# Attention on one Trainium2 core: gathering the plain float32 products into five places a unit

## The chip, the core and the metric

The kernel runs on one core of one Trainium2 chip. The metric is the device time of one launch in microseconds. The engines are TensorE (PE; its weight loads are listed apart as PEld), VectorE (DVE), ScalarE (ACT), GpSimd (POOL) and SyncE (SP), which here issues nearly all DMAs. Each has its own instruction stream, and semaphores are all that orders one against another.

## The reference, cut to what matters

```python
q = xt @ Wq.T                                   # (B, T, D), B 16, T 512, D 256
qh = q.reshape(B, T, NH, dk)                    # 8 heads of 32
scores = scale * einsum('bhqd,bhkd->bhqk', qh, qh)
logits = (scores * cmask + (1.0 - cmask) * NEG) * rmask
attn = softmax(logits, axis=-1)
ctx = einsum('bhqk,bhkd->bhqd', attn, qh)
out = ctx @ Wo.T                                # then a mixture of 8 experts, top 2,
x = x + moe(out) + shared(out) * sigmoid(gate)  # and one shared expert
```

## The kernel before, in words

The program has three parts, one after the other: `attention` (to about 700 us), `experts`, and `shared`. Only `attention` is touched.

Attention works in 32 units: 16 batch entries, two units each, each unit with HG = 4 of the 8 heads. In a unit there are KB = 4 blocks `kb` of 128 keys, and in each block the four heads `g`. A pair (kb, g) issues two products on TensorE: `ps_e` (L557), the scores of unit u, 98 rows deep by 512 columns, and `ps_m` (L562), the same scores the other way round for unit u+2, of which DVE takes the maximum (L420) so that the exponentials of two units later can have it subtracted. Both use float32r operands; high and low parts are stacked in the rows. Each of the two has two PSUM banks, taken in turn: the product of pair t on `ps_e` waits until ACT has made the exponential (L337) of pair t-2, and that on `ps_m` until DVE has reduced pair t-2 (`max_done`, L561).

Between the pairs `step` in the tensor block places by hand all other work of TensorE. A part of it is in plain float32:
- `numerators` (L455), of the block before, at g = 1 of each kb: four products with 32 output rows each, side by side in the array's columns, eight instructions in all; at kb = 0 it is the last block of the unit before;
- `denominators` (L468), the sum of exponentials by a matrix of ones, once for blocks 0 and 1 (g = 3, kb = 3), once for blocks 2 and 3 of the unit before (g = 3, kb = 1);
- `turn_values` (L477), `turn_maxima` (L496) and `turn_rows` (L506), transposes against `ident`;
- `partial_logits` (L514) and `logits` (L521), small products for the gate of the experts.

`turn_rows`, `partial_logits` and `logits` are there in units with even n only. `project` (L485) and `out_rows` (L535, odd n only) are six float32r products each.

The denominators need e[0]+e[1] and e[2]+e[3] added first. `add_pair` (L148) does that: POOL adds all of pair 0 and half of pair 1, DVE the other half of pair 1 (L422), after its reduce of kb 1, g 1; the denominators of pair 1 wait for it (`pair_dve`, L465).

At the end of a unit DVE also has, in its stream: a reciprocal in quarters (L386), two of them in kb 3; the product `c_f` (L391); the small copy `keep_logits` (L430, even n), or, at the head of an even unit, `row_mask` and `row_neg` (L411, L412). Only then do the reduces of the next unit follow.

Of the kernel before, what the change touches and what calls it, by code (L numbers as in the profile page):

```python
def attention(nc, ctx, sems, keep, x, mask, wqT, woT, gates, attn):
# [13 lines left out]
    NU = NB * UPB  # L15
# [88 lines left out]
    def upto(eng, s, value):  # L104

        if not (isinstance(value, int) and value <= 0):
            eng.wait_ge(s, value)
# [27 lines left out]
    def known(i, n, off=0, lo=0, hi=NU):  # L135

        if isinstance(i, int):
            return lo <= RING * i + n + off < hi
        return True
# [234 lines left out]
    @block.vector  # L374
    def _(dve):
        def normalise(i, n, at):

            w, par = RING * i + n - 1, (n - 1) % 2
            if at < 0:
                return  # L380
            if at < PARTS:
                c = slice(at * T // PARTS, (at + 1) * T // PARTS)
                if at == 0:
                    dve.wait_ge(den_done, w + 1)
                    upto(dve, c_done, w)
                dve.reciprocal(den[par][:, c], den[par][:, c]).then_inc(rd_done, 1)  # L386
            elif at == PARTS:
                dve.wait_ge(rd_done, PARTS * (w + 1))
                dve.wait_ge(num_done, w + 1)
                upto(dve, c_split, w - 1)  # L390
                dve.tensor_tensor(c_f[par][:], num[par][:], den[par][:], ALU.mult).then_inc(c_done, 1)  # L391

        dve.memset(one_f[:], 1.0).then_inc(dve_set, 1)
        dve.wait_ge(dve_set, 1)
        dve.tensor_copy(one_row[:], one_f[:]).then_inc(setup, 1)
        dve.wait_ge(w_in, 32)
        dve.tensor_copy(wq_hi[:], wq_f).then_inc(w_split, 1)
        dve.tensor_copy(wo_hi[:], wo_f).then_inc(w_split, 1)
        dve.wait_ge(w_split, 2)
        dve.tensor_tensor(wq_lo[:], wq_f, wq_hi[:], ALU.subtract).then_inc(w_split, 1)  # L400
        dve.tensor_tensor(wo_lo[:], wo_f, wo_hi[:], ALU.subtract).then_inc(w_split, 1)

        def step(i, n):
            u = RING * i + n
            if n % 2 == 0 and known(i, n, 4):
                b, bp = 2 * i + (n + 4) // 2, n // 2
                dve.wait_ge(mask_in[bp], 16 * (i + 2))

                if known(i, n, 1):
                    dve.wait_ge(stack_in[(n + 1) % RING], 16 * STACK_DMAS * (i + (n + 1) // RING + 1))  # L410
                dve.tensor_copy(row_mask[bp][:], mask_b[bp][0:1, :]).then_inc(rows_done, 1)  # L411
                dve.tensor_scalar(row_neg[bp][:], mask_b[bp][0:1, :], -NEG, NEG, ALU.mult, ALU.add).then_inc(rows_done, 1)  # L412
            for kb in range(KB):
                for g in range(HG):
                    if known(i, n, 2):
                        w, par = u + 2, n % 2
                        dve.wait_ge(m_mm, (KB * w + kb) * HG + g + 1)
                        if kb == 0 and g == 0:
                            upto(dve, mt_mm, w - 1)
                        dve.reduce_max(maxcol[par][:, g * KB + kb:g * KB + kb + 1], ps_m[g % 2][:, :], AX.X).then_inc(max_done, 1)  # L420
                    if g == 1 and kb == 1 and known(i, n, -1):
                        add_pair(dve, u - 1, 1, slice(0, HG // 2), pair_dve)  # L422
                    if g % 2 == 1 and known(i, n, -1):
                        normalise(i, n, 2 * kb + g // 2 - KB)
                        if kb == KB - 1 and g == HG - 1:
                            normalise(i, n, PARTS)
                if kb == 3 and n % 2 == 0 and known(i, n, -4, hi=NU):
                    b = 2 * i + (n - 4) // 2
                    dve.wait_ge(lg_mm, b + 1)
                    dve.tensor_copy(keep["logits"][:, bass.ds(KT * b, KT), :],  # L430
                                    ps_o[:, KT * P:KT * (P + NE)].rearrange("p (h e) -> p h e", h=KT)).then_inc(lg_done, 1)

        run_units(dve, step, -4, 5)

    @block.tensor
    def _(pe):
# [10 lines left out]
        def numerators(u, n, kb):  # L447

            if kb == 0:

                upto(pe, num_done, u)
                upto(pe, v_done, u + 1)
            pe.wait_ge(e_done, (KB * u + kb + 1) * HG)
            for g in range(HG):
                last = nc.tensor.matmul(ps_num[g * DK:(g + 1) * DK, :], v[n % RING][:, kb, g, :], e[kb][:, g, :],  # L455
                                        start=(kb == 0), stop=(kb == KB - 1))
            last.then_inc(num_mm, 1)
# [14 lines left out]
        def turn_values(i, n):  # L472

            w, par = RING * i + n + 3, (n + 3) % 2
            pe.wait_ge(q_done, 2 * (w + 1))
            for k in range(KB):
                last = nc.tensor.transpose(ps_q[:, k * P:(k + 1) * P], q_f[par][:, k * P:(k + 1) * P], ident[:, :])  # L477
            last.then_inc(v_mm, 1)
# [9 lines left out]
        def turn_maxima(i, n):  # L488

            upto(pe, max_done, (RING * i + n + 2) * KB * HG)  # L490

            if n % 2 == 0:
                upto(pe, o_done, KT * (2 * i + (n - 4) // 2 + 1))
            else:
                upto(pe, lg_done, 2 * i + (n - 5) // 2 + 1)
            nc.tensor.transpose(ps_o[0:HG * KB, 0:P], maxcol[(n + 1) % 2][:, :], ident[:, :]).then_inc(mt_mm, 1)  # L496
# [41 lines left out]
        def step(i, n):  # L538
            u = RING * i + n
            if isinstance(i, int) and u == 0:  # L540

                pe.wait_ge(ones_in, 16 * RING)
                pe.wait_ge(gate_in, 16)
                pe.wait_ge(add_up_done, KB)
            for kb in range(KB):
                cols = slice(kb * P, (kb + 1) * P)
                if kb == 0 and known(i, n):
                    pe.wait_ge(maxrow_in[n % RING], 16 * (i + 1))
                if kb == 0 and known(i, n, 2):
                    pe.wait_ge(stack_in[(n + 2) % RING], 16 * STACK_DMAS * (i + 1 + (n + 2) // RING))  # L550

                before = ((u - 1, n - 1, KB - 1) if known(i, n, -1) else None) if kb == 0 else ((u, n, kb - 1) if known(i, n) else None)
                for g in range(HG):
                    if known(i, n):
                        tile = (KB * u + kb) * HG + g
                        upto(pe, e_done, tile - 1)
                        nc.tensor.matmul(ps_e[g % 2][:, :], kside[n][:, g, cols], qside[n][:, g, :], start=True, stop=True).then_inc(e_mm, 1)  # L557
                    if known(i, n, 2):
                        s2 = (n + 2) % RING
                        tile = (KB * (u + 2) + kb) * HG + g  # L560
                        upto(pe, max_done, tile - 1)  # L561
                        nc.tensor.matmul(ps_m[g % 2][:, :], qside[s2][0:MAXROW, g, cols], kside[s2][0:MAXROW, g, :], start=True, stop=True).then_inc(m_mm, 1)  # L562
                    if g == 0 and kb == 0 and known(i, n, 3):
                        turn_values(i, n)
                    if g == 0 and kb == 2 and known(i, n, 4):
                        project(i, n)
                    if g == 1 and before:
                        numerators(*before)
                    if g == 2 and kb == 0 and known(i, n, 1):
                        turn_maxima(i, n)  # L570
                    if g == 2 and kb in (1, 2) and n % 2 == 0 and known(i, n, -4, hi=NU):
                        turn_rows(i, n, kb - 1)
                    if g == 0 and kb == 3 and n % 2 == 0 and known(i, n, -4, hi=NU):
                        partial_logits(i, n)
                    if g == 2 and kb == 3 and n % 2 == 0 and known(i, n, -4, hi=NU):
                        logits(i, n)
                    if g == 2 and kb >= 2 and n % 2 == 1 and known(i, n, -3, hi=NU):
                        out_rows(i, n, kb - 2)
                    if g == 3 and kb == 1 and known(i, n, -1):
                        denominators(u - 1, 1)  # L580
                    if g == 3 and kb == 3 and known(i, n):
                        denominators(u, 0)

        run_units(pe, step, -4, 5)

# [821 lines left out]
```

## Time and profile before

| | us |
|---|---|
| median of 3 runs | 2069.23 (2065.56 to 2070.95) |
| span of the profiled execution, first to last instruction | 2067.4 |
| TensorE busy, whole span | 1920.6 (93%) |
| DVE busy, whole span | 1061.5 (51%) |
| TensorE busy between 300 and 400 us | 96.02 of 100 |
| DVE busy between 300 and 400 us | 83.32 of 100 |
| ACT, POOL busy between 300 and 400 us | 68.30, 64.45 of 100 |

The time of the profiled execution itself is not listed; its span stands 1.8 us below the median of the runs. The timeline gives start, duration and instruction; ends of matmuls are modelled and overlap the next start, so the distance from start to start is what a matmul costs. An idle time in square brackets names what ended it.

### The profile page before, as it was taken

The numbers are of one execution on the slowest core, as the hardware profiler recorded it, in microseconds if no ns is written. First come the engines' busy times: TensorE is split into PE (matmuls) and PEld (weight loads), VectorE is DVE, ScalarE is ACT, GpSimd is POOL, SyncE is SP. The second block draws the span as 40 slices with busy tenths as digits, with TensorE's granted clock in tenths as the row PEclk, the third lists the DMA queues.
The fourth block names the chain that finished last, engine by engine and source line by source line (L and its number), as shares of the span: only waits on it lengthen the run. The fifth ranks groups of instructions, "written<-read, shape, count | busy, mean of one in ns | idle before, by whom it ended". The sixth has DMA issues, their size and how long they took to land. (4 is left out here: it accounts for less than half of the span.)

```text
span 2067.4 us, 30281 instructions
## 1 busy us (share of the span) xinstructions
PE 1920.6 (93%) x10324; PEld 1418.9 (69%) x10325; DVE 1061.5 (51%) x1723; ACT 720.1 (35%) x1282; POOL 591.3 (29%) x433
## 2 busy tenths in 40 slices
PE   4999999999999836999999999799999999999996
PEld 2444444444444326999999999688888888888885
DVE  3788888787888455344443443444233332424333
ACT  1566666666666512324343332311101010101100
POOL 3556665666565413111111111001010100101010
PEclk9899999999999956999999999899999999999998
DMA  7765757576765033233332322523030211203021
GB/s 126 120 111 98 113 102 125 92 113 95 131 84 73 21 143 125 81 116 110 123 121 73 114 80 81 169 91 102 1 102 20 81 51 51 67 34 101 0 81 41
DMA packets 103041, 184.22 MB, mean 89 GB/s; under 512 B 10560, under 2 KB 31040, under 8 KB 102992
## 3 DMA queue, kind: packets, MB, share of 16 engines
q1 hardware_dynamic: 91952, 147.41, 32.3%
q0 software_dynamic: 11040, 36.18, 5.9%
q8 instruction: 28, 0.46, 0.1%
q14 instruction: 21, 0.17, 0.0%
HBM read 92.03 MB, written 40.37 MB: 64 GB/s over the span
## 5 line engine op out<-in xcount | busy, mean ns | idle before, releaser
L420 DVE TENSOR_REDUCE maxcol<-ps_m 128x1 f32<-128x512 f32 x512 | 337.5, 681 | 138.8 <-PE ps_m L562 133.1
L337 ACT ACTIVATE e<-ps_e 128x512 f32<-128x512 f32 x512 | 297.0, 596 | 188.4 <-PE ps_e L557 187.6
L1234 DVE TENSOR_TENSOR s_h_f<-s_silu,s_ps_u 128x512 f32<-128x512 f32 x88 | 60.6, 688 | 450.6 <-PE s_ps_u L1290 399.1
L148 POOL TENSOR_TENSOR e<-e 128x2048 f32<-128x2048 f32 x64 | 225.6, 3524 | 181.8 <-ACT e L337 181.5
L1202 ACT ACTIVATE s_silu<-s_ps_g 128x512 f32<-128x512 f32 x88 | 52.6, 598 | 608.1 <-PE s_ps_g L1290 600.5
L562 PE MATMUL ps_m<-kside,qside 97*128 97x512 f32 x512 | 224.7, 444 | 33.2 <-DVE maxcol L420 18.9
L1177 POOL DMA_INDIRECT s_chosen<-routed,s_slot_now x64 | 61.0, 952 | 670.0 <-DVE s_total L1265 659.4
L557 PE MATMUL ps_e<-qside,kside 98*128 98x512 f32 x512 | 237.7, 467 | 3.2 <-ACT e L337 2.4
L557 PEld LDWEIGHTS ps_e<-qside,kside 98*128 98x128 f32 x512 | 97.2, 191 | 192.3 <-ACT e L337 159.1
L964 DVE TENSOR_TENSOR e_h_f<-e_silu,e_ps_h 128x256 f32<-128x256 f32 (+1 forms) x108 | 45.1, 418 | 249.0 <-ACT e_silu L831 249.0
L562 PEld LDWEIGHTS ps_m<-kside,qside 97*128 97x128 f32 x512 | 101.0, 197 | 78.9 <-DVE maxcol L420 53.9
L1290 PE MATMUL s_ps_g<-s_x_hi,s_gu_hi 128*128 128x512 f32 x352 | 138.4, 393 | 3.6 <-DVE s_d_lo L1223 3.6
L455 PE MATMUL ps_num<-e,v 128*32 128x512 f32 x1024 | 137.9, 611 | 0.1
L1290 PE MATMUL s_ps_g<-s_x_lo,s_gu_hi 128*128 128x512 f32 x352 | 137.7, 391 | 0.0
L1301 PE MATMUL s_ps_y<-s_d_hi,s_h_hi 128*128 128x512 f32 x352 | 137.7, 391 | 0.0
L1290 PE MATMUL s_ps_g<-s_x_hi,s_gu_lo 128*128 128x512 f32 x352 | 137.6, 391 | 0.0
L1301 PE MATMUL s_ps_y<-s_d_hi,s_h_lo 128*128 128x512 f32 x352 | 137.1, 389 | 0.0
L1301 PE MATMUL s_ps_y<-s_d_lo,s_h_hi 128*128 128x512 f32 x352 | 136.9, 389 | 0.0
L1290 PE MATMUL s_ps_u<-s_x_hi,s_gu_hi 128*128 128x512 f32 x352 | 136.9, 389 | 0.0
L1290 PE MATMUL s_ps_u<-s_x_lo,s_gu_hi 128*128 128x512 f32 x352 | 136.9, 389 | 0.0
L1290 PE MATMUL s_ps_u<-s_x_hi,s_gu_lo 128*128 128x512 f32 x352 | 136.9, 389 | 0.0
L386 DVE RECIPROCAL den<-den 128x128 f32<-128x128 f32 x128 | 119.5, 939 | 17.0 <-ACT den L268 17.0
(203 smaller groups left out, 4040.8 us busy)
## 6 DMA issues: line engine op xcount, KB each, us to landing
routed<-e_y SPq DMA_DIRECT2D x36, 512.0 KB, 2.8
kside<-q_hi SPq DMA_DIRECT2D x64, 256.0 KB
qside<-qm_hi SPq DMA_DIRECT2D x64, 256.0 KB
x_f<-in_x SPq DMA_DIRECT2D x16, 512.0 KB, 3.4
kside<-q_lo SPq DMA_DIRECT2D x32, 256.0 KB
qside<-qm_lo SPq DMA_DIRECT2D x32, 256.0 KB
attn<-xo SPq DMA_DIRECT2D x32, 256.0 KB, 3.3
keep_rows<-attn SPq DMA_DIRECT2D x8, 1024.0 KB, 5.6
```

Source lines behind the costliest of these rows:

```text
L148: eng.tensor_tensor(into, into, e[k + 1][:, heads, :], ALU.add).then_inc(done, 1)
L337: act.activation(e[kb][:, g, :], ps_e[g % 2][:, :], ACT.Exp, scale=SCALE).then_inc(e_done, 1)
L386: dve.reciprocal(den[par][:, c], den[par][:, c]).then_inc(rd_done, 1)
L420: dve.reduce_max(maxcol[par][:, g * KB + kb:g * KB + kb + 1], ps_m[g % 2][:, :], AX.X).then_inc(max_done, 1)
L455: last = nc.tensor.matmul(ps_num[g * DK:(g + 1) * DK, :], v[n % RING][:, kb, g, :], e[kb][:, g, :], start=(kb == 0), stop=(kb == KB - 1))
L557: nc.tensor.matmul(ps_e[g % 2][:, :], kside[n][:, g, cols], qside[n][:, g, :], start=True, stop=True).then_inc(e_mm, 1)
L562: nc.tensor.matmul(ps_m[g % 2][:, :], qside[s2][0:MAXROW, g, cols], kside[s2][0:MAXROW, g, :], start=True, stop=True).then_inc(m_mm, 1)
L1177: pool.indirect_dma_start(out=chosen[k][s % 2][:], out_offset=None, in_=routed, in_offset=bass.IndirectOffsetOnAxis(ap=slot_now[:, k, s:s ...
L1202: act.activation(silu[:], ps_g[:], ACT.Silu).then_inc(silu_done, 1)
L1234: dve.tensor_tensor(h_f[:], silu[:], ps_u[:], ALU.mult).then_inc(h_done, 1)
L1290: last = nc.tensor.matmul(ps[:], l[:, t, k, m, :], r[:, m, :], start=(c == 0), stop=(c == len(terms) - 1))
L1301: last = nc.tensor.matmul(ps_y[s][:], l[t % 2][:, c], r[:, t, :], start=(t == 0 and m == 0), stop=(t == NI - 1 and m == 2))
```

## The change

On TensorE, what stood alone in the pairs is moved to stand right behind the numerators or the denominators. At g = 1: kb 0 gets `numerators`, `turn_values`, `turn_maxima`; kb 1 gets `numerators`, `denominators` of pair 1, and `turn_rows`; kb 2 `numerators` and `turn_rows`; kb 3 `numerators` and `partial_logits`. At g = 3 of kb 3: `denominators` of pair 0, then `logits`. On DVE its half of `add_pair` moves from behind the reduce of kb 1, g 1 to behind that of kb 0, g 2. Nothing is computed otherwise; no instruction and no DMA is added or removed.

```diff
@@ -418,7 +418,7 @@
                         if kb == 0 and g == 0:
                             upto(dve, mt_mm, w - 1)
                         dve.reduce_max(maxcol[par][:, g * KB + kb:g * KB + kb + 1], ps_m[g % 2][:, :], AX.X).then_inc(max_done, 1)
-                    if g == 1 and kb == 1 and known(i, n, -1):
+                    if g == 2 and kb == 0 and known(i, n, -1):
                         add_pair(dve, u - 1, 1, slice(0, HG // 2), pair_dve)
                     if g % 2 == 1 and known(i, n, -1):
                         normalise(i, n, 2 * kb + g // 2 - KB)
@@ -560,26 +560,28 @@
                         tile = (KB * (u + 2) + kb) * HG + g
                         upto(pe, max_done, tile - 1)
                         nc.tensor.matmul(ps_m[g % 2][:, :], qside[s2][0:MAXROW, g, cols], kside[s2][0:MAXROW, g, :], start=True, stop=True).then_inc(m_mm, 1)
-                    if g == 0 and kb == 0 and known(i, n, 3):
-                        turn_values(i, n)
                     if g == 0 and kb == 2 and known(i, n, 4):
                         project(i, n)
-                    if g == 1 and before:
-                        numerators(*before)
-                    if g == 2 and kb == 0 and known(i, n, 1):
-                        turn_maxima(i, n)
-                    if g == 2 and kb in (1, 2) and n % 2 == 0 and known(i, n, -4, hi=NU):
-                        turn_rows(i, n, kb - 1)
-                    if g == 0 and kb == 3 and n % 2 == 0 and known(i, n, -4, hi=NU):
-                        partial_logits(i, n)
-                    if g == 2 and kb == 3 and n % 2 == 0 and known(i, n, -4, hi=NU):
-                        logits(i, n)
+                    if g == 1:
+                        if before:
+                            numerators(*before)
+                        if kb == 0 and known(i, n, 3):
+                            turn_values(i, n)
+                        if kb == 0 and known(i, n, 1):
+                            turn_maxima(i, n)
+                        if kb == 1 and known(i, n, -1):
+                            denominators(u - 1, 1)
+                        if kb in (1, 2) and n % 2 == 0 and known(i, n, -4, hi=NU):
+                            turn_rows(i, n, kb - 1)
+                        if kb == 3 and n % 2 == 0 and known(i, n, -4, hi=NU):
+                            partial_logits(i, n)
                     if g == 2 and kb >= 2 and n % 2 == 1 and known(i, n, -3, hi=NU):
                         out_rows(i, n, kb - 2)
-                    if g == 3 and kb == 1 and known(i, n, -1):
-                        denominators(u - 1, 1)
-                    if g == 3 and kb == 3 and known(i, n):
-                        denominators(u, 0)
+                    if g == 3 and kb == 3:
+                        if known(i, n):
+                            denominators(u, 0)
+                        if n % 2 == 0 and known(i, n, -4, hi=NU):
+                            logits(i, n)
 
         run_units(pe, step, -4, 5)
```

## Rows read from the trace of the kernel before

**Rows 1.** Busy table of one stretch: TensorE, weight loads, DVE, ACT, POOL, granted clock.
```profile
300.00:400.00 100.00, 96.02 (x510) 47.11 (x509) 83.32 (x115) 68.30 (x126) 64.45 (x33) 0.99 0.66 112
```

**Rows 2.** Timeline of TensorE, end of an odd unit and first half of an even one.
```profile
307.99 0.40 PE L562 MATMUL ps_m<-kside,qside 97*128 97x512 f32 x1
...
313.19 0.50 PE L562 MATMUL ps_m<-kside,qside 97*128 97x512 f32 x1 [0.80 <-DVE maxcol L420]
313.53 0.28 PE L496 MATMUL ps_o<-ident,maxcol 128*16 128x128 f32 x1
...
315.08 0.49 PE L562 MATMUL ps_m<-kside,qside 97*128 97x512 f32 x1
315.54 1.06 PE L455 MATMUL ps_num<-e,v 128*32 128x512 f32 x8
316.54 0.50 PE L557 MATMUL ps_e<-qside,kside 98*128 98x512 f32 x1
316.88 0.39 PE L562 MATMUL ps_m<-kside,qside 97*128 97x512 f32 x1
317.11 0.60 PE L506 MATMUL ps_o<-ident,xo 128*128 128x128 f32 x4
...
318.10 1.07 PE L468 MATMUL ps_den<-e,ones 128*32 128x512 f32 x8
319.10 0.50 PE L557 MATMUL ps_e<-qside,kside 98*128 98x512 f32 x1
```

**Rows 3.** Timeline of DVE, the same stretch and the rest of the unit.
```profile
310.01 1.86 DVE L391 TENSOR_TENSOR c_f<-num,den 128x512 f32<-128x512 f32 x1
...
312.47 3.85 DVE L420 TENSOR_REDUCE maxcol<-ps_m 128x1 f32<-128x512 f32 x6
316.23 1.22 DVE L148 TENSOR_TENSOR e<-e 128x1024 f32<-128x1024 f32 x1
...
323.38 0.69 DVE L420 TENSOR_REDUCE maxcol<-ps_m 128x1 f32<-128x512 f32 x1
...
332.65 3.84 DVE L420 TENSOR_REDUCE maxcol<-ps_m 128x1 f32<-128x512 f32 x6
```

**Rows 4.** Timeline of TensorE, later in the same unit and in the next.
```profile
325.27 0.64 PE L514 MATMUL ps_o<-xo_t,gate_w 128*32 128x256 f32 x8 [0.57 <-ACT xo_t L315]
...
328.07 0.51 PE L521 MATMUL ps_o<-add_up,partial 128*128 128x9 f32 x4
...
328.75 0.40 PE L562 MATMUL ps_m<-kside,qside 97*128 97x512 f32 x1
...
333.38 0.51 PE L562 MATMUL ps_m<-kside,qside 97*128 97x512 f32 x1 [0.22 <-DVE maxcol L420]
...
344.55 0.40 PE L562 MATMUL ps_m<-kside,qside 97*128 97x512 f32 x1
...
346.16 1.06 PE L455 MATMUL ps_num<-e,v 128*32 128x512 f32 x8
...
354.58 0.51 PE L562 MATMUL ps_m<-kside,qside 97*128 97x512 f32 x1 [0.81 <-DVE maxcol L420]
```

**Rows 5.** TensorE where its clock fell (timeline, busy table), and other idle times.
```profile
147.66 0.50 PE L562 MATMUL ps_m<-kside,qside 97*128 97x512 f32 x1 [0.84 <-DVE maxcol L420]
...
395.94 0.51 PE L562 MATMUL ps_m<-kside,qside 97*128 97x512 f32 x1 [0.80 <-DVE maxcol L420]
...
398.43 1.94 PE L455 MATMUL ps_num<-e,v 128*32 128x512 f32 x8
...
399.00:400.00 1.00, 1.00 (x8) 0.00 (x0) 1.00 (x2) 0.96 (x1) 0.00 (x0) 0.50 1.09 131
...
417.66 0.51 PE L562 MATMUL ps_m<-kside,qside 97*128 97x512 f32 x1 [0.22 <-DVE maxcol L420]
...
604.07 0.49 PE L562 MATMUL ps_m<-kside,qside 97*128 97x512 f32 x1 [0.72 <-DVE maxcol L420]
...
682.82 0.99 PE L557 MATMUL ps_e<-qside,kside 98*128 98x512 f32 x2 [1.19 <-ACT e L337]
```

## The prediction, made before the changed kernel had run

> **What bounds the kernel now.** I read the busy table first [rows 1]: between 300 and 400 us TensorE is busy 96 of 100 us at a granted clock of 0.99, DVE 83. So TensorE sets the pace, and at first sight every tenth of a microsecond that it saves counts. The timeline then says where this fails [rows 2, 4]. Call M the start of the last `ps_m` product of a unit (kb 3, g 3) and T that of the next unit's third (kb 0, g 2). M is at 307.99, T at 313.19, and T ends 0.80 us in which TensorE was idle until DVE had reduced an older tile. The next T, 333.38, waited 0.22; the one after, 354.58, waited 0.81. A unit from an even T to an odd one thus takes 20.19 us, one from odd to even 21.20. The even stall is there all along the loop: in 12 such rows, first 147.66, last 604.07 [rows 5].
>
> The timeline of DVE gives the reason [rows 3]. Behind M it has a reduce, a reciprocal, `c_f` (1.86 us) and small copies before the six reduces that start at 312.47. They run back to back, 0.63 us apart (3.85 us for six), so DVE is a full tile queue behind. T follows the start of the first by 0.72 us (313.19 less 312.47), and every `ps_m` product follows the reduce two tiles before it so: the product of kb 1, g 1 at 315.08 answers to the fourth, which started at 312.47 + 3 x 0.63 = 314.36. So from M to that product DVE is the bound, and TensorE only behind it.
>
> **The part that adds: `add_pair` on DVE.** It takes 1.22 us and holds the next reduce back by 1.13 (316.23 plus 1.13 is 317.36, where TensorE, in bursts, did not want it) [rows 3]. It now stands behind the third of the six reduces, ahead of the fourth. With R the start of the first: third R+1.26, add R+1.90, fourth R+3.03 where it was R+1.89; so the `ps_m` product of kb 1, g 1 starts at R+3.75, which is T+3.03, against T+1.89 now. All that TensorE issues behind it waits: the numerators, denominators and everything later. The numerators start at T+2.35 now, 0.46 behind that product, some of it a wait for ACT's copy of `ps_num` (which will be done by then); without it 0.33 behind, T+3.36. **Plus 1.01 to 1.05 a unit.** The inputs of the add are ready there, since the last exponentials of the unit before are older than T. Where it stood it held nobody up, so nothing is given back.
>
> **What merging saves.** A plain float32 burst of numerators or denominators goes 1.00 us from its start to the next product (315.54 to 316.54, 318.10 to 319.10), and the pair behind it is 0.34 apart, where products following smoothly are 0.23 apart (316.88 to 317.11) [rows 2]. Four passes of 0.23 are 0.92, so an edge costs 0.08 in the burst, 0.11 behind it, and up to 0.1 ahead of it: at most 0.3 an island, worked out from these rows, at least nothing. The trace has no two such bursts in a row. I take 0.27 for the denominators put behind numerators of the same form, and nothing for the transposes, whose operands fill the whole width and which keep their own time.
> The Trainium skill ("TensorEngine Tiling (Array Packing)", Key Properties) says that a change of tiling mode drains the engine; numerators use a quarter of the columns, transposes all of them, so by that rule the edge stays inside the cluster. The 0.08 inside a burst agrees, no row shows the edge between the two. Without the rule each transposing step would give about another 0.1.
>
> Taken away, between numerators and the next kb there are now rows of three or four pairs without anything long. The two banks then bind: the row of 344.55 to 346.16, two and a half pairs, took 1.61 us where five steps of 0.23 are 1.15 [rows 4]. A burst in the middle of a row hides that latency; at its end it does not.
>
> **Sum for an odd unit** (T to T, nothing but kb 0 and kb 1 changes): +1.04; denominators behind numerators -0.27; the row of three pairs behind them, kb 1 g 2 to kb 2 g 0, held by the reduces, +0.2. **+0.97**, bounds 0.88 and 1.14.
> **Even unit:** the same +0.97. The wait of `partial_logits` for ACT's `xo_t` (0.57 idle, 0.7 with what it does to the weight load) goes, since a numerator burst now stands ahead [rows 4]: -0.7. Its own edge: -0.1. `logits` moves behind M: it starts at 328.07 and M at 328.75, 0.68 on, where 0.23 would do [rows 4]: -0.45. Its new place is in the stretch that DVE binds, M to T 4.63 here, 5.20 at an even T. TensorE's own work in it becomes 4.6, so it costs nothing there. But kb 2 g 2 to kb 3 g 1 is now a row of four pairs, with `q_hi` on ACT between their exponentials: +0.8. That makes +0.5. DVE bounds this from below: from its reduce at 323.38 (kb 2, g 2) to R at 332.65 it takes 9.27 us [rows 3], of which some 1.0 is waiting for products; with these closed up the unit could shrink by 0.05 at best. **+0.5**, bounds -0.05 and +0.9.
> `turn_values` and `turn_maxima` at kb 0 lie ahead of T, so inside what DVE binds: nothing gained or lost (`turn_maxima` needs `lg_done`, set just before R, and stands some 0.6 ahead of T). On SP and POOL nothing changes its place; `qside<-maxrow` follows the same copy on ACT.
> There are 29 units with both the add and `ps_m` products (units 1 to 29): 14 x 0.5 + 15 x 0.97 = 21.5, less a half for the first, where DVE is behind for another reason: **+21**, bounds +12 and +30.
>
> **The clock.** Near 398 the granted clock fell to 0.50 of full speed, 1.2 GHz [rows 5]: the numerators at 398.43 took 1.94 us, and T to T took 21.72 (395.94 to 417.66) against 20.19. This came after an even T with its 0.80 idle, in 1 of 12; after the idle 1.19 at 682.82 the clock fell too. The change puts 1.1 us of idling at T+1.9, less than 2 us behind the old one. So I expect falls in a third of the 29 units, an estimate between 1 and about 20: 10 x 1.53 = **+15**, bounds 0 and +30.
> The Trainium skill ("TensorE: Matmul & The Clock Gate", "Why this matters for your kernels") asks only that TensorE avoid idle gaps much longer than these between bursts; by that rule nothing falls, and the sum is the +21 alone. The row at 398 disagrees.
>
> **The time.** Span 2067.4 + 21 + 15 = 2103.4; the median of the runs is 1.8 above the span: **2105**.
>
> **The rivals.**
> 1. As forecast, the add delays kb 1 and the clock falls now and then: 2096 to 2128. Chance 0.60.
> 2. The add delays, the clock holds: 2069 + 12 to 27, about 2090, range 2080 to 2096. For it: 11 of 12 stalls of 0.8 did no harm. 0.20.
> 3. The clock falls in nearly all units: 21 + 29 x 1.53 = +65, 2134. For it: the one idle time over a microsecond that the rows show at this density had its fall. 0.06.
> 4. Faster. On average 9.5 islands a unit become 5. If each of the 4.5 is worth the full 0.3, that is 1.35 a unit against 1.04 lost, and the wait of `partial_logits` goes on top: 29 x 0.31 + 14 x 0.7 = 19, about 2050. It decides from 1.04 / 4.5 = 0.23 an island upwards. Against it: three or four of them lie in the stretch that DVE binds, where no saving of TensorE's arrives. 0.09.
> 5. It does nothing measurable: the reduces have slack that I overlook and the rows of pairs eat the merging. 0.05.
>
> **The numbers.** The range 2080 to 2128 holds cases 1 and 2 and leaves out 3 and 4. A measurement of this kernel tells about 0.3% (6 us) from no change. Slower by more: 0.86; within: 0.05; faster by more: 0.09.
>
> **What would show it.** In the trace after: an idle time of 1 to 1.2 us ahead of `ps_m` at kb 1, g 1, released by a reduce, in each unit, with `add_pair` of DVE between the third and fourth reduce; T to numerators 3.3 to 3.4; M to T still 5.2 at an even T; no idle time ahead of `partial_logits`; numerators and denominators together 1.9; numerators of 1.9 us alone where the clock was down, ten or so. The prediction is wrong if the reduces do not wait behind the add, or if numerators with transposes behind them take clearly less than apart.

## The result and the profile after

The changed kernel takes 2115.04 us (median of 4 runs, 2113.4 to 2116.31) against 2068.91 before (also 4 runs): a ratio of 1.0226, 95% interval 1.0212 to 1.024. It is 46 us slower. The forecast was 2105 in a range of 2080 to 2128. The profiled execution has a span of 2112.6 us, 1.8 below its time of 2114.4, so 45.2 more than before. 43 of them have come together by unit 29, the last of the loop with both products: its T is at 663.21 before and at 706.14 now.

The first line of the page, and the busy table from 300 to 400 us (TensorE, weight loads, DVE, ACT, POOL, granted clock):

```profile
PE 1944.3 (92%) x10324; PEld 1424.2 (67%) x10325; DVE 1058.4 (50%) x1723; ACT 714.3 (34%) x1282; POOL 591.8 (28%) x433
```

```profile
300.00:400.00 100.00, 93.59 (x488) 45.16 (x488) 78.39 (x110) 63.08 (x121) 60.48 (x31) 0.97 0.62 98
```

Against [rows 1] TensorE is busy less of the time (93.6 of 100 us), and its mean granted clock is 0.97 where it was 0.99. Both terms of the forecast are in these two figures: it waits more, and it runs slower now and then.

The timeline of TensorE, two units; T as in the prediction is the first product of each group (308.55 odd, 330.75 even, 353.08 odd):

```profile
308.55 0.40 PE L562 MATMUL ps_m<-kside,qside 97*128 97x512 f32 x1
...
311.47 0.49 PE L562 MATMUL ps_m<-kside,qside 97*128 97x512 f32 x1 [1.00 <-DVE maxcol L420]
311.90 1.06 PE L455 MATMUL ps_num<-e,v 128*32 128x512 f32 x8
...
312.78 1.04 PE L468 MATMUL ps_den<-e,ones 128*32 128x512 f32 x8
...
313.75 0.50 PE L557 MATMUL ps_e<-qside,kside 98*128 98x512 f32 x1
...
330.75 0.50 PE L562 MATMUL ps_m<-kside,qside 97*128 97x512 f32 x1 [0.75 <-DVE maxcol L420]
...
333.76 0.61 PE L562 MATMUL ps_m<-kside,qside 97*128 97x512 f32 x1 [0.99 <-DVE maxcol L420]
...
334.30 1.94 PE L455 MATMUL ps_num<-e,v 128*32 128x512 f32 x8
...
336.01 1.73 PE L468 MATMUL ps_den<-e,ones 128*32 128x512 f32 x8
...
337.68 0.66 PE L506 MATMUL ps_o<-ident,xo 128*128 128x128 f32 x4
...
338.09 0.48 PE L557 MATMUL ps_e<-qside,kside 98*128 98x512 f32 x1
...
346.11 1.06 PE L455 MATMUL ps_num<-e,v 128*32 128x512 f32 x8
346.99 0.61 PE L514 MATMUL ps_o<-xo_t,gate_w 128*32 128x256 f32 x8
...
351.25 1.06 PE L455 MATMUL ps_num<-e,v 128*32 128x512 f32 x8
...
352.24 0.66 PE L477 MATMUL ps_q<-ident,q_f 128*128 128x128 f32 x4
...
353.08 0.40 PE L562 MATMUL ps_m<-kside,qside 97*128 97x512 f32 x1
```

DVE in the even one:

```profile
330.02 1.95 DVE L420 TENSOR_REDUCE maxcol<-ps_m 128x1 f32<-128x512 f32 x3
...
331.89 1.22 DVE L148 TENSOR_TENSOR e<-e 128x1024 f32<-128x1024 f32 x1
...
333.03 2.08 DVE L420 TENSOR_REDUCE maxcol<-ps_m 128x1 f32<-128x512 f32 x3
```

In the even unit the product at kb 1, g 1 stands at T+3.01 (333.76 less 330.75), where [rows 2] has T+1.89, and in the odd one at T+2.92 (311.47 less 308.55); 1.00 and 0.99 us of idling stand ahead of it in the odd and the even unit, both ended by a reduce. The odd T is 0.09 nearer to it because it no longer waits for DVE: TensorE's own work from M to it now takes 4.74 us, where DVE made it 4.63 before. The product itself answers to DVE in both. DVE's three reduces, the add and then the fourth reduce are 330.02, 331.89, 333.03: R, R+1.87, R+3.01. An odd and an even unit together, T to T, take 44.53 us (308.55 to 353.08) where it was 41.39 [rows 2, 4]. The odd unit takes 22.20 (308.55 to 330.75; before 21.20), the even one 22.33 (before 20.19). In the even one numerators and denominators took 1.94 and 1.73 against 1.06 and 1.04: there the clock was down. The busy table of the same microseconds says so, with the granted clock third from the end:

```profile
333.00:334.00 1.00, 0.23 (x1) 0.19 (x1) 1.00 (x3) 1.00 (x3) 0.00 (x0) 1.00 1.07 135
...
335.00:336.00 1.00, 1.00 (x8) 0.20 (x4) 0.10 (x1) 0.00 (x0) 0.00 (x0) 0.50 1.11 139
...
338.00:339.00 1.00, 1.00 (x8) 0.74 (x5) 0.17 (x1) 0.40 (x1) 0.00 (x0) 1.00 1.15 143
```

### The profile page after: what moved, and what is told of

It is laid out like the page before. It is cut to its first block and busy times, and to the rows that moved or that the text cites. A ratio compares the mean times of both kernels' runs of the same rounds, so it can differ in the third digit from the quotient of the medians.

```text
span 2112.6 us, 30281 instructions
## 1 busy us (share of the span) xinstructions
PE 1944.3 (92%) x10324; PEld 1424.2 (67%) x10325; DVE 1058.4 (50%) x1723; ACT 714.3 (34%) x1282; POOL 591.8 (28%) x433
## 5 line engine op out<-in xcount | busy, mean ns | idle before, releaser
L337 ACT ACTIVATE e<-ps_e 128x512 f32<-128x512 f32 x512 | 288.4, 598 | 236.8 <-PE ps_e L557 235.6
L562 PE MATMUL ps_m<-kside,qside 97*128 97x512 f32 x512 | 231.0, 455 | 58.2 <-DVE maxcol L420 44.4
L557 PE MATMUL ps_e<-qside,kside 98*128 98x512 f32 x512 | 229.0, 450 | 6.0 <-ACT e L337 3.8
L966 DVE TENSOR_TENSOR e_h_f<-e_silu,e_ps_h 128x256 f32<-128x256 f32 (+1 forms) x108 | 45.2, 418 | 249.5 <-ACT e_silu L833 249.5
L455 PE MATMUL ps_num<-e,v 128*32 128x512 f32 x1024 | 149.9, 660 | 0.1
```

The costliest lines, as they stand in the source:

```text
L337: act.activation(e[kb][:, g, :], ps_e[g % 2][:, :], ACT.Exp, scale=SCALE).then_inc(e_done, 1)
```

## The experiments

A pair of units here means T to T over two units in the steady middle of the loop, from the timeline of TensorE.

**1. The move on DVE alone.** The kernel before, with
```diff
-                    if g == 1 and kb == 1 and known(i, n, -1):
+                    if g == 2 and kb == 0 and known(i, n, -1):
                         add_pair(dve, u - 1, 1, slice(0, HG // 2), pair_dve)
```


> The kernel before, with only DVE's half of add_pair moved behind the reduce of kb 0, g 2; TensorE's order is that of before. Theory (the add holds the fourth reduce back, and the idle time it makes lets the clock fall): 29 units x 1.04 us = +30, plus one fall of the clock in each of 14 even units at 1.5 us = +21, so 2120, range 2108 to 2128; idle of about 1.0 us ahead of ps_m at kb 1, g 1. Rival (the clusters of plain float32 products on TensorE are what costs): close to before, 2069 to 2080.


Measured: 2130.55 us, ratio 1.0305 (1.0285 to 1.0324), 2.5 us above the range. So the move of one instruction on DVE, with TensorE's order untouched, costs more than the whole change.

```profile
334.77 0.50 PE L562 MATMUL ps_m<-kside,qside 97*128 97x512 f32 x1 [0.80 <-DVE maxcol L420]
...
337.79 0.80 PE L562 MATMUL ps_m<-kside,qside 97*128 97x512 f32 x1 [0.98 <-DVE maxcol L420]
...
338.52 1.93 PE L455 MATMUL ps_num<-e,v 128*32 128x512 f32 x8
...
358.81 0.51 PE L562 MATMUL ps_m<-kside,qside 97*128 97x512 f32 x1 [0.22 <-DVE maxcol L420]
```

Again 1.0 us of idling at T+3.02. A pair of units without a fall of the clock takes 43.6 us, 2.2 more than before, twice 1.1. With a fall it takes 46.4 here: this fall lasts longer than those of the changed kernel (slow products from 337.79 to 342.68) and costs 2.7 us; in an odd unit such a one costs 3.0. Units 1 to 29 have 13 stretches of slow products against 2 before, some of them short ones at 1.6. From T of unit 1 to T of unit 29 the loop is 57 us longer than before: 28 x 1.1 = 31 are the waiting, which leaves 26 for the falls. The estimate had 51 in all, and 62 were measured.

**2. TensorE's order alone.** The changed kernel with that DVE line back at kb 1, g 1.


> The changed kernel, with DVE's add_pair back behind the reduce of kb 1, g 1; TensorE's order is the changed one. The denominators of pair 1 then wait for the add: they start near T+4.4 where the changed kernel has T+4.24. Theory: the same loss of time from waiting, +0.16 us a unit on top, but the idle time now follows eight products and a burst, so the clock falls in few units or none: about 2115 - 21 + 5 = 2098, range 2090 to 2108. Rival (the clock is no separate term, waiting is all): 2115 + 5 = 2120. Rival (the add's place is all that costs): back to 2069 or below.


Measured: 2090.51 us, ratio 1.0109 (1.0092 to 1.0126), at the lower end of the range.

```profile
321.49 0.50 PE L562 MATMUL ps_m<-kside,qside 97*128 97x512 f32 x1 [0.73 <-DVE maxcol L420]
...
323.81 1.06 PE L455 MATMUL ps_num<-e,v 128*32 128x512 f32 x8
...
325.88 1.07 PE L468 MATMUL ps_den<-e,ones 128*32 128x512 f32 x8 [1.00 <-DVE e L148]
```

The waiting has only moved: the denominators, straight behind the numerators, wait 1.00 us for DVE's add. A pair takes 43.07 us, 1.7 more than before. But the clock stays up all through the loop but at 107 and 237 us. The difference to the changed kernel is that the products from T on follow with small gaps only and the idle time comes behind a whole burst; that this is the reason was not tried by itself. As much waiting as in the changed kernel, and 25 us less, near the 22 that its falls make (below). The rival without a term for the clock (2120) falls, and so does the one that blamed the add's place for all.

**3. Filling the new idle time.** The changed kernel with the scores product of kb 1, g 1 issued four times.
```diff
+                        for _ in range(3 if (kb, g) == (1, 1) else 0):
+                            nc.tensor.matmul(ps_e[g % 2][:, :], kside[n][:, g, cols], qside[n][:, g, :], start=True, stop=True)
                         nc.tensor.matmul(ps_e[g % 2][:, :], kside[n][:, g, cols], ...).then_inc(e_mm, 1)
```


> The changed kernel, with the ps_e product of kb 1, g 1 issued four times (same operands, same bank, only the last counts), which fills 0.7 of the 1.0 us of idling ahead of ps_m at kb 1, g 1 and delays nothing that is waited for. Theory: the clock no longer falls in even units, 14 x 1.55 = -22, so 2093, range 2090 to 2100. Rival (the slow bursts are not due to the idling): 2115 or a little more.


Measured: 2098.18 us, ratio to before 1.0143 (1.0125 to 1.016).

```profile
300.00:400.00 100.00, 96.70 (x516) 49.40 (x513) 78.75 (x110) 64.58 (x120) 60.09 (x29) 1.00 0.69 106
```

```profile
325.91 0.50 PE L564 MATMUL ps_m<-kside,qside 97*128 97x512 f32 x1 [0.73 <-DVE maxcol L420]
...
327.54 0.87 PE L558 MATMUL ps_e<-qside,kside 98*128 98x512 f32 x3
...
328.93 0.50 PE L564 MATMUL ps_m<-kside,qside 97*128 97x512 f32 x1 [0.29 <-DVE maxcol L420]
...
329.36 1.07 PE L455 MATMUL ps_num<-e,v 128*32 128x512 f32 x8
...
330.24 1.04 PE L468 MATMUL ps_den<-e,ones 128*32 128x512 f32 x8
```

The product still starts at T+3.02; nothing waits less. But numerators take 1.07 and denominators 1.04 now, the granted clock from 300 to 400 us is 1.00 (the first line, of the busy table), units 2 to 29 have one stretch of slow products, at the head of unit 2 (110 to 114), and a pair of units takes 42.90 us against 44.53. Three useless products a unit save 17 us in all. From T of unit 1 to T of unit 29 they save 21.5; the 5.5 lost again lie outside those units, half of them ahead of unit 1 and half behind unit 29. What is left against before, 1.5 a pair, is the waiting less what merging saves, and it is what the prediction's unit sums gave (0.97 + 0.5).

**4. Filling the old idle time.** The same three extra products at kb 0, g 2, in even units only (`3 if (kb, g) == (0, 2) and n % 2 == 0 else 0`).


> The changed kernel, with the ps_e product of kb 0, g 2 issued four times in even units only: it fills 0.69 of the 0.75 us of idling ahead of T there and leaves the 1.0 us ahead of kb 1, g 1 as it is. Theory (it is both idle times together, 2 us apart, that let the clock fall; odd units have only the second and no falls): no falls in the loop, 2115 - 17 = 2098, as when the second is filled, range 2094 to 2103. Rival (the longer idle time at kb 1 alone does it, something else differs in odd units): 2113 to 2118.


Measured: 2111.69 us (2103.39 to 2113.87), ratio 1.0198 (1.0174 to 1.0222): between the two forecasts, and near the rival's.

```profile
330.84 0.50 PE L564 MATMUL ps_m<-kside,qside 97*128 97x512 f32 x1
...
333.86 0.67 PE L564 MATMUL ps_m<-kside,qside 97*128 97x512 f32 x1 [1.00 <-DVE maxcol L420]
...
334.46 1.94 PE L455 MATMUL ps_num<-e,v 128*32 128x512 f32 x8
```

T at 330.84 has no idle time ahead of it any more, and the clock fell all the same. In the profiled execution (2113.87 us, the slowest of the four) no product was slow between 426 and 596 us, and there was a fall in most even units outside: 12 falls in the loop against 16 in the changed kernel. So my theory that the two idle times act only together does not hold: filling the first makes falls fewer at best. From unit 6 to unit 28 the changed kernel has its falls in even units alone, though the odd ones have the same 1.00 us of idling; three more are in the odd units 1, 5 and 29, and experiment 1 has some in odd units too (at 268.74 and 405.47). Why they strike where they do is open.

**5. Denominators and add where they were, the rest gathered.** The changed kernel with
```diff
-                        if kb == 1 and known(i, n, -1):
-                            denominators(u - 1, 1)
+                    if g == 3 and kb == 1 and known(i, n, -1):
+                        denominators(u - 1, 1)
```
and DVE's add at kb 1, g 1.


> The changed kernel, with both the denominators of pair 1 (kb 1, g 3) and DVE's add_pair (kb 1, g 1) where they were before; the transposes, partial_logits and logits stay gathered. Theory: odd units as before, even ones -0.45 us (no wait of partial_logits -0.7, its edge -0.1, logits behind M -0.45, the row of four pairs +0.8): 2069 - 6 = 2063, range 2056 to 2069. Rival (gathering costs more than it saves, whatever the add does): 2075 to 2090.


Measured: 2057.84 us, ratio 0.9947 (0.9928 to 0.9965): 0.5% faster than before, clear of the noise. A pair takes 40.61 us (311.89 to 352.50).

```profile
311.89 0.50 PE L562 MATMUL ps_m<-kside,qside 97*128 97x512 f32 x1 [0.76 <-DVE maxcol L420]
...
324.46 1.06 PE L455 MATMUL ps_num<-e,v 128*32 128x512 f32 x8
...
325.34 0.61 PE L514 MATMUL ps_o<-xo_t,gate_w 128*32 128x256 f32 x8
...
352.50 0.50 PE L562 MATMUL ps_m<-kside,qside 97*128 97x512 f32 x1 [0.73 <-DVE maxcol L420]
```

`partial_logits` follows the numerators by 0.88 us and waits for nobody. The pair gains 0.8 us, not 0.45 (T to T 0.65 of it in the even unit, 0.13 in the odd). Gathering the rest thus helps a little, and the whole loss came with moving the denominators of pair 1 and the add that they need.

**6. `partial_logits` alone** moved behind the numerators of kb 3, g 1, in the kernel before.


> The kernel before, with partial_logits alone moved behind the numerators of kb 3, g 1. Theory: the 0.57 us wait for ACT goes (-0.7 with its weight load), its own edge -0.1, against a row of two pairs more (kb 2 g 3 to kb 3 g 1, turn_rows still in it) at 0 to +0.4: -0.4 to -0.8 in 14 to 16 even units, 2069 - 9 = 2060, range 2055 to 2064. Rival (the wait only moves to the banks of ps_e): 2067 to 2071.


Measured: 2061.25 us, ratio 0.9968 (0.9958 to 0.9979), as forecast; a pair takes 40.86. So 0.5 of the 0.8 us is this one step. Its trace has no wait ahead of `partial_logits` any more: the burst of numerators covers the wait for ACT, and a saved edge is worth 0.1 of it at most by the estimate.

**7 and 8. POOL adds all of pair 1.** DVE's half and the wait on `pair_dve` are taken away, in the changed kernel and in the kernel before.
```diff
-                add_pair(pool, u - 1, 1, slice(HG // 2, HG), pair_pool)
+                add_pair(pool, u - 1, 1, slice(0, HG), pair_pool)
```


> The changed kernel, with POOL adding all of pair 1 (DVE's half gone from DVE, 1.22 us less there, POOL's add 4.59 instead of 2.38 us, ready near T+0.3 and so before the denominators need it). Theory (the place of DVE's add is all that makes the change slow, the gathering itself saves): no idle time at kb 1, g 1, no falls there; a pair of units 42.9 - 2 x 1.04 = 40.8 or less against 41.38 before, so 2056, range 2048 to 2064. Rival (den1 at kb 1, g 1 makes rows of pairs that cost more than its edge): 2065 to 2080. Rival (POOL's longer add slows c_f on DVE): T later by the lengthening of c_f, up to 1.7 us a unit, 2100.

> The kernel before, with POOL adding all of pair 1. DVE's add stood where nobody waited for it, so theory: no change, 2062 to 2072. Rival (POOL's longer add slows c_f): slower, and the same amount as in the changed kernel with POOL adding all.


Measured: 2164.75 us (1.0471, 1.0454 to 1.0489) and 2175.73 us (1.0518, 1.0501 to 1.0536). Both are far slower and far outside their ranges, though DVE has less to do. The timelines of experiment 7, DVE's, POOL's and TensorE's:

```profile
337.78 4.03 DVE L391 TENSOR_TENSOR c_f<-num,den 128x512 f32<-128x512 f32 x1
```

```profile
336.71 4.55 POOL L148 TENSOR_TENSOR e<-e 128x2048 f32<-128x2048 f32 x1
```

```profile
343.13 0.50 PE L558 MATMUL ps_m<-kside,qside 97*128 97x512 f32 x1 [2.93 <-DVE maxcol L420]
```

`c_f` on DVE took 4.03 us and ended 0.5 behind POOL's add, which had started before it. T waited 2.93 us for it. `c_f` has 512 elements a partition, and DVE's own add of 1024 takes 1.22. So the 1.86 us of `c_f` in [rows 3], which I had taken as its price, was mostly this: beside POOL's add of 2.38 us it ends half a microsecond behind that. The idle times ahead of T before the change come from there (experiment 10, below, has none). The rival that foresaw this gave 2100; the loss is greater. In experiment 8 T waits 2.39 and 2.97 us (odd, even), where it was 0.22 and 0.80 [rows 2, 4]: 2.2 in each unit, 29 x 2.2 = 64 of the 107 us lost, with falls of the clock on top, which the estimate had left out. The rival's "same amount" did not hold for experiment 7, which lost 50 on the changed kernel: there the wait for DVE's own add goes at the same time. The two runs end 11 us apart, about what experiment 5 gained by gathering.

**9 to 11. POOL's add behind `c_lo`.** So that POOL's half of the add no longer runs beside `c_f`:
```diff
-            if known(i, n, -1):
-                add_pair(pool, u - 1, 1, slice(HG // 2, HG), pair_pool)
             if known(i, n, -2):
                 ...  # c_lo
+            if known(i, n, -1):
+                add_pair(pool, u - 1, 1, slice(HG // 2, HG), pair_pool)
             if known(i, n):
                 add_pair(pool, u, 0, slice(0, HG), pair_pool)
```
in the kernel of experiment 5 (9), in the kernel before (10), and in the changed one (11).


> den1_and_add_back, and on POOL its half of add_pair for pair 1 moved behind c_lo, so that it no longer runs beside c_f on DVE. Theory (c_f, 1.8 us beside POOL's add of 2.4, 3.9 beside one of 4.6, at least 0.69 alone, waits out POOL's add): c_f falls to about 0.7, the first reduce of the unit comes 1.1 earlier, TensorE binds M to T: even T -0.95, odd T 0; 14 x -0.95 = -13 from 2058, so 2044, range 2038 to 2050. Rival (c_f is slow by itself, or waits for something else): 2056 to 2060. Rival (the denominators of pair 1 then wait for POOL): 2060 to 2075.

> The kernel before, with the same move on POOL alone. Theory: even T -0.95, odd T -0.39 (4.63 to TensorE's own 4.24), so 14.5 x -1.34 = -19, 2049, range 2043 to 2056. Rivals as for the run beside it: 2066 to 2070, or slower.

> The changed kernel, with the same move on POOL. DVE's add, now behind the reduce of kb 0, g 2, meets POOL's add there. Theory: c_f is short again, but DVE's add of 1.2 takes 2.5 or more, so the product of kb 1, g 1 starts near T+4.6 instead of T+3.0; with T 0.4 to 0.95 earlier the pair of units is 2 us longer: 2115 + 32 = 2147, range 2125 to 2160. Rival (two adds do not hinder one another, only c_f was hindered): T earlier by 1.1 twice a pair and the rest as it is, 2085.


Measured: 2041.02 us (0.9866, 0.985 to 0.9883), 2044.11 us (0.9887, 0.987 to 0.9903) and 2175.33 us (1.0525, 1.0508 to 1.0543). The estimates were 2044, 2049 and 2147; the third time is outside its range. The first kernel, DVE, POOL and TensorE:

```profile
318.06 0.69 DVE L391 TENSOR_TENSOR c_f<-num,den 128x512 f32<-128x512 f32 x1
```

```profile
321.05 2.38 POOL L148 TENSOR_TENSOR e<-e 128x1024 f32<-128x1024 f32 x1
```

```profile
340.67 0.40 PE L562 MATMUL ps_m<-kside,qside 97*128 97x512 f32 x1
```

`c_f` takes 0.69 us, and the even T, 340.67, waits for nobody, where experiment 5 has 0.76 and 0.73 us of idling ahead of it. In the second kernel neither T waits any more. The third, DVE, POOL and TensorE:

```profile
322.21 2.90 DVE L148 TENSOR_TENSOR e<-e 128x1024 f32<-128x1024 f32 x1
```

```profile
321.64 2.38 POOL L148 TENSOR_TENSOR e<-e 128x1024 f32<-128x1024 f32 x1
```

```profile
321.16 0.40 PE L562 MATMUL ps_m<-kside,qside 97*128 97x512 f32 x1
...
325.76 0.51 PE L562 MATMUL ps_m<-kside,qside 97*128 97x512 f32 x1 [2.67 <-DVE maxcol L420]
```

There `c_f` is short as well, but now DVE's add meets POOL's, takes 2.90 us instead of 1.22 and ends 1.1 behind it, and TensorE waits 2.67. The changed kernel has its add in just the stretch in which POOL's must not be. The product of kb 1, g 1 stands at T+4.60 (321.16 to 325.76), as forecast. That run still came out 28 us above the estimate. From 60 us to the last numerators its clock fell 26 times, that of the other two kernels once each; that the 28 us come from there is inferred, not tried.

## Why the prediction was right, point by point

- **DVE is the bound from M to kb 1, g 1, and the add delays its fourth reduce.** Forecast: T+3.03, idling of 1 to 1.2 us in each unit, +1.01 to 1.05. Measured: T+3.01 in the even unit, T+2.92 in the odd one, T+3.02 in experiment 1; idling 0.98 to 1.02 in nearly every unit. From the first reduce R the add is at R+1.87 and the fourth reduce at R+3.01 (forecast R+1.90, R+3.03). Experiments 1 and 2 show it from both sides. One reading was slightly off: TensorE's own work between M and an odd T was put at 4.6 us, within what DVE binds, and is 4.74, so there TensorE sets T. It costs nothing, since DVE still sets the product at kb 1, g 1.
- **The unit sums.** Forecast +0.97 odd, +0.5 even, +21 in all. Measured: odd +1.00 (22.20 less 21.20); both together without falls +1.5 (experiment 3), so +0.5 even. The parts of the even unit were not measured one by one. The 45.2 us less the falls (below) leave 23.
- **What merging saves.** Denominators behind numerators: forecast 1.9 us together and 0.27 saved. Measured: 0.88 and 0.97, 1.85 us (311.90 to 313.75), so the second burst adds 0.85, where alone it added its 1.00 and 0.2 of edges: 0.35 saved, a little more than forecast and than the bound of 0.3 an island. Transposes behind numerators: nothing forecast, and 0.41 us to the next product (337.68 to 338.09) where 0.35 stood before (317.11 to 317.46); against the edge ahead of them that goes, about nothing. By the Trainium skill ("TensorEngine Tiling (Array Packing)", Key Properties), which has a change of tiling drain the engine, this was to be expected; the trace agrees: the numerators ahead of transposes keep their 0.99 us (351.25 to 352.24), those ahead of `partial_logits`, which uses the columns in the same way, take 0.88 (346.11 to 346.99).
- **The clock: the term mis-sized.** Forecast 10 falls at 1.53, +15. Measured: in the profiled executions the clock fell 16 times in units 1 to 29 against 2 before (one of the 2 beside an idle time of 3.99 us at the loop's start, the other is that of [rows 5]). The price was right: pairs of 44.53 with a fall and 42.90 without (experiment 3) give 1.6. 14 x 1.6 = 22. The count was an estimate between 1 and 20, and is at its upper end. These 7 us, and 2 of the waiting, are the gap from 2105 to 2115. That the time lies in the range all the same is owed to the width given to this term, 0 to +30, and not to its reason. What I gave as the reason, two idle times close together, is not borne out as such (experiment 4); that the new one is at the root is (experiment 3, where filling it took the falls away). The Trainium skill's advice on idle gaps ("TensorE: Matmul & The Clock Gate", "Why this matters for your kernels") would have had no falls at gaps of 1.0 us; these runs disagree with it.
- **`partial_logits`.** Its wait of 0.57 is gone, as forecast. The row of four pairs ahead of it costs less than the 0.8 taken, perhaps 0.4 to 0.5, inferred from experiment 5 (a pair gains 0.8 where 0.45 was forecast) on the assumption that the other terms are right.
- **The rivals.** Without falls: experiment 3 makes that case and takes 2098; its mechanism is real, its number was not the outcome. Faster: it needed 0.23 us an island; the one island that saves has 0.35, the transposes nothing, and what lay ahead of T was hidden as said. (By the kernel's text there are 12 islands in an even unit and 8 in an odd one, so 10 on average become 5, not 9.5; the limit is then 0.21, and the outcome of this rival is the same.)
- **A step that held by luck.** I took `c_f` for a piece of DVE's own work of fixed length. Most of it is a wait for POOL (experiments 7 to 11). It had the same neighbour in both kernels (1.86 us before, 1.75 after ahead of the odd T), so the sum did not suffer; had the change moved anything on POOL, it would have.

## What to carry to other kernels

When a step is moved to let another engine start sooner, look at what queues behind it on its own engine: 1.1 us of work put into a backlog of two-buffer hand-overs is paid by everyone downstream, and where it had stood it was free. A long instruction with a small operand is to be suspected before it is accepted: compare its time per element with its neighbours', and see which other engine is busy for just as long. Idle time on TensorE costs a second time where it pulls the clock down (here 1.0 us of waiting and 1.6 of slow products); filling it with useless products shows how much of a loss is the clock.

## What the runs showed of the hardware

- In these kernels a `tensor_tensor` of DVE on two SBUF operands did not run beside one of POOL: `c_f` took 0.69 us alone, 1.8 beside 2.38 us of POOL, 3.9 beside 4.55; DVE's add 1.22 alone and 2.90 beside 2.38. The Trainium skill ("SBUF — State Buffer", "SBUF: two separate sides") says it: DVE with two operands in SBUF and a POOL instruction reading SBUF exclude each other for a whole instruction, and the later one waits. The trace agrees: `c_f` of [rows 3] started at 310.01, 1.07 us behind POOL's add (below, 308.94 to 311.32), and ended 0.55 after it. No semaphore orders the two, though the text on the chip at the head names semaphores as all that orders engines, and the profile shows the instruction that is held up as busy and long, with no idle time ahead of it. DVE's reduces out of PSUM kept their 0.63 to 0.69 beside the same adds. POOL's add before, and `c_f` grouped between 100 and 600 us in the kernel before, in experiment 8 and in experiment 9:

```profile
308.94 2.38 POOL L148 TENSOR_TENSOR e<-e 128x1024 f32<-128x1024 f32 x1
```

```profile
L391 DVE TENSOR_TENSOR c_f<-num,den 128x512 f32<-128x512 f32 x24 | 43.5, 1811 | 1.3
```

```profile
L391 DVE TENSOR_TENSOR c_f<-num,den 128x512 f32<-128x512 f32 x21 | 81.5, 3879 | 1.2
```

```profile
L391 DVE TENSOR_TENSOR c_f<-num,den 128x512 f32<-128x512 f32 x26 | 18.8, 724 | 1.4
```

- Moving one POOL instruction past another, with nothing else changed, gave 24 us (2044.11 against 2067.91), and with experiment 5's order 27 (2041.02). The difference between these two, 3 us, was not measured for itself; both beat the kernel before and the changed one.
- Idle times of about 1 us brought the granted clock from 2.4 to 1.2 GHz in some units (slow products in the changed kernel from 333.8 to 337.7, in experiment 1 from 337.8 to 343), and three products of 0.2 us in the gap kept it at 1.00 of full speed (experiment 3). The same 1.0 us brought no fall in most odd units of the changed kernel, and in experiment 2, straight behind a burst, two falls in the whole loop.
